# Local attention blocks: probabilities placed by DMAs, the keys' rotated sum on VectorE, query squares folded by GpSimd

## What is computed

```
qkv = x @ Wqkv;  q, k, v = split(qkv, 3), 16 heads of 64
q = l2norm(q) * qs;  k = l2norm(k) * ksc
q = q * cos * scale + rotate_half(q) * sin * scale
k = k * cos / scale + rotate_half(k) * sin / scale
# a window of 32 queries sees the 32 keys before it and its own 32
sim  = q_window . (k_previous, k_own) * 8, masked outside the band
attn = softmax(sim)
out  = (attn . (v_previous, v_own)) @ Wo;  then an MLP with a gate
```

## Time and profile before

| | |
|---|---|
| median of 3 runs | 3162.67 us (3152.88 to 3163.48) |
| the profiled execution | 3146.83 us |
| its span, first to last instruction | 3144.8 us |
| busy in the span | PE 2774.6, DVE 2442.2, ACT 2104.3, POOL 1351.6 us |
| mean granted TensorE clock | 0.954 |

### The profile page before, as it was taken

One profiled execution on the slowest core, in us unless ns is written; L12 is line 12 of the kernel. 1 busy time (PEld: TensorE's weight loads), 2 busy tenths in 40 slices (PEclk: granted clock), 3 DMA queues, 4 the chain that ended last, 5 costly groups with the idle time before them and its releaser, 6 DMA issues. The chain is left out here.

```text
span 3144.8 us, 72108 instructions
## 1 busy us (share of the span) xinstructions
PE 2774.6 (88%) x27244; PEld 1692.0 (54%) x27244; DVE 2442.2 (78%) x3071; ACT 2104.3 (67%) x3079; POOL 1351.6 (43%) x1209
## 2 busy tenths in 40 slices
PE   5799999997678989888889898989999999789997
PEld 3122222223546565656566666656665656478885
DVE  3899999992379797979798888888888979455554
ACT  2488888885158787878788787878787878311111
POOL 1000000000078685867586758676766767200000
PEclk7799999998589999999999999999999999889998
DMA  3011111100010001000100010001000000000001
GB/s 131 27 29 28 28 29 29 29 24 8 8 57 9 6 9 43 7 8 9 42 9 6 17 34 9 8 15 36 8 7 14 15 7 9 12 18 0 0 0 34
DMA packets 56465, 64.35 MB, mean 20 GB/s; under 512 B 24742, under 2 KB 38964, under 8 KB 55348
## 3 DMA queue, kind: packets, MB, share of 16 engines
q1 hardware_dynamic: 55380, 60.58, 7.0%
q10 hardware_dynamic: 864, 0.79, 0.1%
HBM read 36.69 MB, written 7.34 MB: 14 GB/s over the span
## 5 line engine op out<-in xcount | busy, mean ns | idle before, releaser
L886 DVE TENSOR_REDUCE a_minus_max<-a_ps_max 128x1 f32<-128x1024 f32 x512 | 596.8, 1218 | 57.6 <-PE a_ps_max L811 52.3
L794 ACT ACTIVATE a_expT<-a_ps_scoresT 128x512 f32<-128x512 f32 (+1 forms) x683 | 528.8, 808 | 78.2 <-PE a_ps_scoresT L829 67.4
L1178 POOL TENSOR_TENSOR b_turned_q<-b_rot_q,b_turned_q 128x1024 f32<-128x1024 f32 x96 | 226.8, 2362 | 270.2 <-DVE b_turned_q L1549 257.3
L844 PE MATMUL a_ps_out<-a_expT,v_aug 128*32 128x256 f32 x4096 | 327.9, 392 | 5.4 <-ACT a_outT L781 4.8
L1620 DVE STREAM_TRANSPOSE b_probsT<-b_probs 32x512 f32<-32x512 f32 x384 | 269.4, 702 | 11.9 <-POOL b_probs L1219 0.3
L765 POOL CAST a_max_hi<-a_minus_max 128x16 bf16<-128x16 f32 x32 | 6.3, 198 | 631.1 <-DVE a_minus_max L886 631.1
L1287 ACT ACTIVATE b_kT<-b_psD 64x512 f32<-64x512 f32 x384 | 226.1, 589 | 58.6 <-PE b_psD L1374 53.5
L829 PE MATMUL a_ps_scoresT<-a_q_op,a_k_op 26*128 26x512 bf16 x1024 | 247.2, 385 | 13.1 <-ACT a_expT L794 4.4
L1225 POOL TENSOR_TENSOR b_turned_k<-b_rot_k,b_turned_k 128x512 f32<-128x512 f32 x192 | 243.9, 1270 | 0.2 <-DVE b_turned_k L1549 0.2
L1185 POOL TENSOR_TENSOR b_rot_q<-b_turned_q,b_inv_norm 128x1024 f32<-128x1024 f32 x96 | 182.8, 1904 | 137.7 <-issue 137.7
L1219 POOL TENSOR_TENSOR b_probs<-b_probs,b_inv_sum 128x512 f32<-128x512 f32 x192 | 197.3, 1049 | 99.1 <-DVE b_inv_sum L1593 99.1
(11 more groups left out here) (295 smaller groups left out, 6019.4 us busy)
## 6 DMA issues: line engine op xcount, KB each, us to landing
b_v_edge<-b_v SPq DMA_DIRECT2D x96, 128.0 KB
b_w_qkv<-L_ffn_Wqkv SPq DMA_DIRECT2D x6, 1536.0 KB
a_q_op<-terms_q SPq DMA_DIRECT2D x128, 48.0 KB
a_k_op<-terms_k SPq DMA_DIRECT2D x128, 48.0 KB
joined<-a_outT SPq DMA_DIRECT2D x256, 16.0 KB
b_w_o<-L_ffn_Wo SPq DMA_DIRECT2D x6, 512.0 KB
a_q_op<-a_max_rows SPq DMA_DIRECT2D x128, 4.0 KB
b_w<-L_ffn_W SPq DMA_DIRECT2D x6, 341.0 KB
```

The costliest lines, as they stand in the source:

```text
L794: act.activation(expT[:, to:to + 512 * size], ps_scoresT[:, at:at + 512 * size], ACT.Exp, scale=SCALE_A).then_inc(exp_ready, 1)
L844: last_mm = pe.matmul(ps_out[lo:lo + 32, 256 * part:256 * part + 256], v_aug[:, b * T8 + kt, head, :], expT[:, at:at + 256], start=(kt == ...
L886: dve.tensor_reduce(minus_max[p % 2][:, side, 0, qt:qt + 1], ps_max[u % 2][:], AX.X, ALU.max, negate=True).then_inc(max_taken, 1)
L1178: pool.tensor_tensor(turned[:], rot[:], turned[:], ALU.add).then_inc(added, 1)
```

## The change

1. The own keys' blocks are transposed by one instruction into a new tensor, `packed_own`. Four DMAs bring `packed` to `edgeT` and `probsT`, four more bring `packed_own` to `probsT`, each 32 partitions of 2 KB. The copies by ScalarE and GpSimd go. `probsT` is laid out as (4, heads, 32) so that a block is one run; the value product reads it in four pieces of 32.
2. The sum of the keys' rotation moves from GpSimd (two halves) to VectorE (one instruction, right behind the sine product).
3. GpSimd adds the query squares of a head, 64 to 32 to 16, and VectorE sums the 16. VectorE does the cosine and sine products of the queries ahead of that sum, not behind it.
4. The next layer's Wqkv comes in six DMAs of 256 KB, one in each of six steps of a layer's first batch.

The diff, cut to its core:

```diff
         packed = sb("packed", [P, HEADS_B, W])
-        probsT = sb("probsT", [P, HEADS_B, P])
+        packed_own = sb("packed_own", [P, HEADS_B, W])
+        probsT = sb("probsT", [P, P // W, HEADS_B, W])
...
         @block.sync
+            def load_qkv_part(l, slot, part):
+                at = slot * 3 * INNER + part * 512
+                sp.dma_start(w_qkv[:, ds(at, 512)], wts["Wqkv"][ds(l, 1), :, ds(part * 512, 512)].rearrange("o p n -> p (o n)")).then_inc(w_qkv_in, 16)
...
+                if 1 in lags:
+                    sp.wait_ge(packed_ready, T)
+                    if 2 in lags:
+                        sp.wait_ge(out_half, 2 * (T - 1))
+                    sp.dma_start(edgeT[P - W:P], packed[0:W]).then_inc(back_placed, 16)
+                    for j in range(1, P // W):
+                        sp.dma_start(probsT[W * j - W:W * j, j], packed[W * j:W * j + W]).then_inc(back_placed, 16)
+                    sp.wait_ge(packed_own_ready, T)
+                    for j in range(P // W):
+                        sp.dma_start(probsT[W * j:W * j + W, j], packed_own[W * j:W * j + W]).then_inc(own_placed, 16)
+                if b == 0 and not isinstance(s, int) and not (isinstance(l, int) and l == LAST):
+                    load_qkv_part(l + 1, (l + 1) % 2, s - 2)
...
         @block.gpsimd
-                    for j in (2, 3):
-                        rows = slice(W * j, W * j + W)
-                        pool.tensor_tensor(probsT[W * j - W:W * j, :, rows], packed[rows], ones[rows].unsqueeze(2).to_broadcast([W, HEADS_B, W]),
-                                           ALU.mult).then_inc(high_back_ready, 1)
...
+                    squares = square_q[:].rearrange("p (h d) -> p h d", d=DH)
+                    pool.wait_ge(square_q_ready, T + 1)
+                    for n, width in enumerate((32, 16)):
+                        pool.tensor_tensor(squares[:, :, 0:width], squares[:, :, 0:width], squares[:, :, width:2 * width], ALU.add).then_inc(square_q_folded, 1)
...
-                    pool.wait_ge(parts_k_ready, 2 * T + 2)
+                    pool.wait_ge(sum_k_ready, T + 1)
                     for half in range(2):
                         heads = slice(8 * half, 8 * half + 8)
-                        pool.tensor_tensor(turned_k[:, heads], rot_k[:, heads], turned_k[:, heads], ALU.add).then_inc(sum_k_ready, 1)
...
         @block.scalar
-                    act.activation(edgeT[P - W:P], packed[0:W], ACT.Copy).then_inc(low_back_ready, 1)
-                    act.activation(probsT[0:W, :, W:2 * W], packed[W:2 * W], ACT.Copy).then_inc(low_back_ready, 1)
...
         @block.tensor
-                    pe.wait_ge(probsT_ready, 4 * (T - 1))
-                    pe.wait_ge(low_back_ready, 2 * (T - 1))
-                    pe.wait_ge(high_back_ready, 2 * (T - 1))
+                    pe.wait_ge(own_placed, 64 * (T - 1))
+                    pe.wait_ge(back_placed, 64 * (T - 1))
...
         @block.vector
-                    dve.wait_ge(norm_ready, T)
-                    squared_norm(square_q, square_q_ready, 0)
+                    dve.wait_ge(square_q_ready, T + 1)
                     rotary_cos(psQ, rot_q, parts_q_ready, qT_half, 0)
                     rotary_sin(psQ, turned_q, parts_q_ready, 0)
+                    dve.wait_ge(norm_ready, T)
+                    dve.wait_ge(square_q_folded, 2 * T + 2)
+                    dve.tensor_reduce(norm2[:, 0:HEADS_B], square_q[:].rearrange("p (h d) -> p h d", d=DH)[:, :, 0:16], AX.X, ALU.add).then_inc(norm2_ready, 1)
...
+                    dve.wait_ge(parts_k_ready, 2 * T + 2)
+                    dve.tensor_tensor(turned_k[:], rot_k[:], turned_k[:], ALU.add).then_inc(sum_k_ready, 1)
...
-                    for j in range(P // W):
-                        rows = slice(W * j, W * j + W)
-                        dve.transpose(probsT[rows, :, rows], probs[rows, :, 1, :]).then_inc(probsT_ready, 1)
+                    if 2 in lags:
+                        dve.wait_ge(own_placed, 64 * (T - 1))
+                    dve.transpose(packed_own[:], probs[:, :, 1, :]).then_inc(packed_own_ready, 1)
```

More of the change, by code:

```diff
@@ L984, in local_blocks @@
         square_k_ready = sem("square_k_ready")
+        square_q_folded = sem("square_q_folded")
         norm2_ready = sem("norm2_ready")
@@ L1007, in local_blocks @@
         packed_ready = sem("packed_ready")
-        probsT_ready = sem("probsT_ready")
-        low_back_ready = sem("low_back_ready")
-        high_back_ready = sem("high_back_ready")
+        packed_own_ready = sem("packed_own_ready")
+        back_placed = sem("back_placed")
+        own_placed = sem("own_placed")
         out_half = sem("out_half")
@@ L1109, in step @@
             def step(l, b, s, par, lags, ahead=None):
+                T = l * TILES + b * T8 + s
                 if 0 in lags:
-                    T = l * TILES + b * T8 + s
                     sp.wait_ge(v_held, 2 * T + 2)
                     sp.dma_start(v_edge[par][P - W:P, :], v[1 - par][P - W:P, :]).then_inc(v_edge_in, 16)
+                if 1 in lags:
[10 more added lines that the diff above has]
+                    load_qkv_part(l + 1, (l + 1) % 2, s - 2)
             def middle(l, b):
@@ L1139, in _ @@
             load_mlp(0)
+            sp.wait_ge(zeroed, 9)
             stream(sp, step, middle)
@@ L1148, in _ @@
             pool.memset(edgeT[:], 0.0).then_inc(zeroed, 1)
-            pool.memset(ones[:], 1.0).then_inc(zeroed, 1)
             for i in range(2):
                 pool.memset(v_edge[i][:], 0.0).then_inc(zeroed, 1)
-            pool.wait_ge(zeroed, 8)
+            pool.wait_ge(zeroed, 7)
             for b in range(BATCHES):
                 pool.memset(y[64:P, column(b * T8):column(b * T8) + 1], 0.0).then_inc(zeroed, 1)
-            pool.wait_ge(zeroed, 10)
+            pool.wait_ge(zeroed, 9)
             def tokens_of(t, par):
@@ L1239, in _ @@
         def _(act):
-            act.wait_ge(zeroed, 10)
+            act.wait_ge(zeroed, 9)
             def norm_start(l, b, n):
@@ L1337, in _ @@
         def _(pe):
-            pe.wait_ge(zeroed, 10)
+            pe.wait_ge(zeroed, 9)
             def mean(l, b, n, ended):
@@ L1363, in step @@
                 if isinstance(s, int) and s == 0 and b == 0 and 0 in lags:
-                    pe.wait_ge(w_qkv_in, 16 * (l + 1))
+                    pe.wait_ge(w_qkv_in, 16 + 16 * 6 * l)
                 w_at = l % 2 * 3 * INNER
@@ L1434, in step @@
                                 at = P * (pair % 4)
-                                pe.matmul(psD[half][rows, at:at + P], v[par][:, DH * head:DH * head + DH], probsT[:, head, :],
+                                pe.matmul(psD[half][rows, at:at + P].rearrange("p (j w) -> p j w", w=W), v[par][:, DH * head:DH * head + DH], probsT[:, :, head, :],
                                           start=(pair % 4 == 0), stop=False, skip_group_check=True)
@@ L1514, in _ @@
         def _(dve):
-            dve.wait_ge(zeroed, 10)
+            dve.wait_ge(zeroed, 9)
             def centre(l, b, n):
@@ L1572, in step @@
                     if 2 in lags:
-                        dve.wait_ge(probsT_ready, 4 * (T - 1))
+                        dve.wait_ge(packed_own_ready, T - 1)
                     rows = probs[:].rearrange("p h c k -> p h (c k)")
@@ L1610, in step @@
                     if 2 in lags:
-                        dve.wait_ge(low_back_ready, 2 * (T - 1))
-                        dve.wait_ge(high_back_ready, 2 * (T - 1))
-                        dve.wait_ge(out_half, 2 * (T - 1))
+                        dve.wait_ge(back_placed, 64 * (T - 1))
                     dve.transpose(packed[:], probs[:, :, 0, :]).then_inc(packed_ready, 1)
@@ L1617, in step @@
                     dve.wait_ge(probs_ready, 2 * T)
-                    for j in range(P // W):
-                        rows = slice(W * j, W * j + W)
-                        dve.transpose(probsT[rows, :, rows], probs[rows, :, 1, :]).then_inc(probsT_ready, 1)
-                        if j == 0 and ahead:
-                            scale(ahead[0], ahead[1], 0)
+                    if 2 in lags:
+                        dve.wait_ge(own_placed, 64 * (T - 1))
+                    dve.transpose(packed_own[:], probs[:, :, 1, :]).then_inc(packed_own_ready, 1)
+                    if ahead:
+                        scale(ahead[0], ahead[1], 0)
                 elif ahead:
```

14 lines of the change are left out of this document (1 added, 13 removed).

## The result

The changed kernel takes 3249.36 us, the median of four runs (3241.65 to 3259.64), against 3157.78 for the kernel before in the same comparison: a ratio of 1.0304, 95% interval 1.0264 to 1.0344. It is slower by 3%, where I forecast 1.6% faster; 3249 also lies above the range of 3090 to 3200. The time is that of the second rival, the loop of the DMAs (3244).

The account below looks back on a forecast made before the run. VectorE was taken as the bound before (15.94 us a step), TensorE's round through ScalarE after (15.33): 84 x 0.61 = 51 us off 3146.8 gives 3095.6, or 3111 against the median; range 3090 to 3200.

Parts of the forecast that it names:

- the second rival: Placements by DMA: their loop becomes the bound, 16.77 us a step with the scalings' 0.90 inside, 3244 us; chance 0.20.
- the loop of the DMAs: From one value product through exponential, reciprocal, key sum, transpose and eight placements to the next: 15.0 us, bounds 14.1 to 16.5.
- round of 15.33: TensorE's round with the chain through ScalarE, 10.72 + 4.61 us, taken to set the plain step after the change.
- The key sum, put at 1.22: VectorE's add of two SBUF operands after the sine product: 1.22 us, or 1.35 with 0.13 of waiting for that product.
- The first rival: VectorE's key sum waits for GpSimd's scalings and starts 0.90 us later: 3173 us, within 0.5%; chance 0.23.
- The placements, 5.75: Eight placements on SyncE's queue: 7 x 0.55 + 1.9 = 5.75 us from first issue to last landing.
- the eight stores in the earlier trace: Stores in a row at L734, 8 rows of SBUF each: pitch 0.67 us, taken as upper bound for the placements' pitch.
- The value product in four pieces of 32: TensorE reading the probabilities in four pieces of 32 columns: no cost taken; a tenth slower would be 17 us in all.
- The reduced query sum: VectorE's sum of query squares, cut from 1024 to 256 elements a partition: from 1.22 to 0.424 us, so -0.80.
- VectorE's own need: VectorE's work in a plain step after the change: 15.94 - 2.23 - 0.80 + 1.35 = 14.26 us.
- The folds "just fit": GpSimd's folds end at 1570.4, VectorE needs them at 1570.5; a miss up to 1.07 us costs nothing.
- The MLP steps, nothing gained or lost: In steps with an MLP the key sum ends at 1494.60 against 1494.58 for VectorE's z add: no change in time.

Follow-up runs that it names:

- add_waits: The changed kernel with VectorE told to wait by semaphore for both of GpSimd's scalings before the key sum: 3283.79 us, ratio 1.0429 to the kernel before.
- add_only: The kernel before with only the key sum moved to VectorE: 3288.73 us in one run, against 3148.14 before.
- late_add: The changed kernel with VectorE's key sum moved behind the first transpose (in MLP steps behind the norm's scaling): 3097.73 us, ratio 0.9828 to the kernel before.
- extra_dma: The changed kernel with a ninth placement, into a buffer that nothing reads, ahead of the eight: 3320.38 us, ratio 1.0538 to the kernel before.
- dma_only: The kernel before with only the placements by DMA and the weights in six parts: 3147.22 us, ratio 0.9996 to the kernel before.
- late_add_nofold: late_add without GpSimd's folds, VectorE summing all 64 query squares: 3093.99 us, ratio 0.9812 to the kernel before.

## Why the prediction was wrong

- **The loop of the DMAs was the step that failed.** The prediction had it at 15.0 us, "hidden, barely", under a round of 15.33. It measures 16.59. Two terms were too small, by 0.68 and 0.79; the other 0.11 is the transpose.
- **The key sum, put at 1.22 with no wait for GpSimd.** From the sine product to the transpose it is 3.22 for 2.54. The first rival had the wait, at 0.90, and its place right; the runs show 0.84 (add_waits), without any placement too (add_only), and that moving the sum takes it out of the loop (late_add). It had 0.23 as a case of its own. The Trainium skill, "SBUF — State Buffer", section "Who interferes with whom", was named beside that rival: who began first keeps the port. The rows agree: GpSimd's second scaling began at about 1606.55, the sum at 1606.61, and the sum ends 1.08 behind the scaling, here as in the other 726.
- **The placements, 5.75.** They take 6.54. I took the issue of a lone DMA, 0.51, and put 0.55 with the gap. In a run only the first costs that; the pitch is 0.62 to 0.64 (extra_dma: +0.64), near the 0.67 of the eight stores in the earlier trace rows that I had called an upper bound. The landing was 2.19 up to the value product for 1.9. Row for row the nearer case was the run of eight, not the DMA of equal size. By its bounds for pitch and landing, 4.87 to 7.19, the 6.54 is inside; the loop's 14.1 to 16.5 missed 16.59 because the key sum had no bound.
- **The second rival's 3244** holds both prices. Its step (16.77) is 0.18 high and its MLP intervals (+11 us) are 28 too low; the 70 us of its plain steps were 48, since those after an MLP gain 0.61 and the others lose 0.74 on average, 0.66 in the usual one. The two errors nearly cancel, so the nearness to 3249 is partly luck. I had weighed its two halves as if they were rare together (0.20); the overlap and the pitch were both in the rows. Two slips in the sums decide nothing: the first rival's 15.9 is 0.03 below the step of before and not 0.01, and with 0.2 more on the loop it comes to 3190, not to the range's 3200.
- **The round of 15.33 was right.** late_add shows it in nearly every plain step, and the changed kernel behind each MLP. The value product in four pieces of 32 costs nothing: 1.09 for 1.09. The reduced query sum is 0.42, as taken from the earlier trace rows.
- **VectorE's own need, 14.26 a step.** Right: in late_add it idles 0.23 + 0.56 + 0.42 of 15.33, which leaves 14.1. But VectorE was not the only bound before, as the prediction had it (dma_only).
- **The folds "just fit".** They miss by 0.56 in late_add, within the 1.07 that I had left, and cost nothing (late_add_nofold).
- **The MLP steps, nothing gained or lost.** Wrong: +39 us. I looked at VectorE's z add alone and not at the value product, which waits 0.76 to 2.15 for the placements there, nor at the clock.

## What to carry to other kernels

Before an operation with two SBUF operands goes to VectorE, see what GpSimd does at that moment, and ask what stands behind it: the 0.84 us of waiting is two thirds of the 1.26 by which the loop passes the round of 15.33 (without it the loop would be 15.75, an estimate from 16.59), and moving one instruction behind the next turned a loss of 3% into a gain of 1.7%. Price a run of DMAs on one queue by a row of a run, its last landing included, and write such a chain down as a loop of its own, because a margin of 0.3 us under the bound is less than what two estimates of it can miss. And an engine that seems the bound may have a chain of the same length beside it: unloading VectorE alone gained nothing.

## What the runs showed of the hardware

- A VectorE sum of two SBUF operands that meets a GpSimd scaling under way shows as a long instruction (2.07 for 1.23), not as idle time. It ends 1.08 us behind the scaling however much of it lies beside it (0.15 to 1.03 us, 727 cases), and the scaling is not slowed (1.05). Waiting for the scaling by semaphore makes it 1.33.
- 64 KB from SBUF to SBUF in one DMA take 0.51 us of SyncE's queue as the first of a run and 0.59 behind another (0.62 to 0.64 with the gap), and land 1.9 to 2.0 us after the issue at the median; single ones take up to 1.72 and land after up to 3.7. A part of the weights behind them, four times as large, takes 0.35.
- In one MLP TensorE's granted clock went from 1.00 to 0.70 behind a wait of 1.93 us and was 0.50 over the gate's products; with the wait cut to 0.36 the same place kept 1.00. Elsewhere it held behind 2.10 us, and at the gate's products it fell without such a wait in 5 of 11 MLPs before the change.
